# ScalarE makes the first-layer activation two units ahead, before the unit's messages; raw rounding and constant rows come after the messages

## The reference

```python
h = relu(layernorm(x))                       # no weights
e = relu(raw @ W_e1.T + b_e1) @ W_e2.T + b_e2   # raw: (206250, 64)
edge_emb = (e * (clip(polarity, 0, 1) + 0.01)) @ W_le.T + b_le
msg  = relu(h[src] + edge_emb)
aggr = segment_sum(msg, dst, 6250)
g = (h + aggr) @ W_g1.T + b_g1
out = x + relu(layernorm(g) * ln_g + ln_b) @ W_g2.T + b_g2
```

## Time and profile before

| | |
|---|---|
| median of 3 runs | 2511.51 us |
| profiled execution / its span | 2513.17 / 2511.5 us |
| TensorE busy (matmuls) | 2341.1 us, 93% |
| VectorE busy | 1904.1 us, 76% |
| GpSimd busy | 1644.0 us, 65% |
| ScalarE busy | 1586.8 us, 63% |
| second layer, L828, TensorE | 1467.2 us |
| TensorE idle ahead of L806 (first layer) | 129.2 us |

### The profile page before, as it was taken

One profiled execution on the slowest core, in us unless ns is written; L12 is line 12 of the kernel. 1 busy time (PEld: TensorE's weight loads), 2 busy tenths in 40 slices (PEclk: granted clock), 3 DMA queues, 4 the chain that ended last, 5 costly groups with the idle time before them and its releaser, 6 DMA issues.

```text
span 2511.5 us, 34919 instructions
## 1 busy us (share of the span) xinstructions
PE 2341.1 (93%) x10492; PEld 1946.3 (77%) x10492; DVE 1904.1 (76%) x3747; ACT 1586.8 (63%) x3112; POOL 1644.0 (65%) x1679
## 2 busy tenths in 40 slices
PE   5798999999999999999999999999999999999998
PEld 4677787877887787778877787877787787787876
DVE  7677777877787777777777777777787777777776
ACT  7566666666666666666666666666666666666664
POOL 6666666666666666666666666666666666666663
PEclk9899999999999999999999999999999999999999
DMA  9444444444444444444444444444444444444442
GB/s 311 131 132 129 132 146 131 139 130 134 145 140 136 131 145 139 135 133 141 139 136 133 133 135 143 134 137 132 137 143 137 134 134 143 137 137 134 141 140 60
DMA packets 136344, 349.07 MB, mean 139 GB/s; under 512 B 32019, under 2 KB 58325, under 8 KB 136149
## 3 DMA queue, kind: packets, MB, share of 16 engines
q0 software_dynamic: 77376, 211.39, 29.6%
q1 hardware_dynamic: 58772, 135.37, 15.8%
HBM read 333.82 MB, written 12.82 MB: 138 GB/s over the span
## 4 chain that ended last, share of the span: by engine, by line
PE 50%; DVE 27%; another core or an unknown queue 9%; issue 9%; ACT 4%; POOL 1%; DVEq 0%; DMA 0%; ACTq 0%; SPq 0%
PE bank L828 29%; DVE bank L676 11%; PE bank L844 9%; DVE mhl L686 7%; PE bank L806 5%; DVE oh L665 4%; PE bank L807 4%; DVE rlo L427 3%; ACT mhl L601 1%; PE bank L875 1%; PE bank L861 1%; ACT rhi L422 1%; POOL x_sba L371 1%; ACT hh L589 1%
## 5 line engine op out<-in xcount | busy, mean ns | idle before, releaser
L578 POOL DMA_INDIRECT hx<-gather_table,sidx x1612 | 1604.9, 996 | 823.7 <-issue 400.6
L828 PE MATMUL bank<-wc,hh 128*128 128x256 f32 x6448 | 1467.2, 380 | 2.7 <-issue 2.5
L828 PEld LDWEIGHTS bank<-wc,hh 128*128 128x128 f32 x6448 | 1218.9, 191 | 179.8 <-issue 9.2
L601 ACT ACTIVATE mhl<-bank 128x512 fp32r<-128x512 f32 x806 | 482.3, 599 | 842.1 <-DVE bank L676 671.7
L676 DVE SCALAR_TENSOR_TENSOR bank<-bank,gt,hx 128x256 f32<-128x256 f32 x1612 | 683.0, 484 | 380.1 <-remote 311.1
L686 DVE SCALAR_TENSOR_TENSOR mhl<-bank,mhl 128x512 fp32r<-128x512 f32 x806 | 549.7, 689 | 26.8 <-ACT mhl L601 1.8
L806 PE MATMUL bank<-rhi,w1r 128*128 128x512 f32 x806 | 379.8, 471 | 129.2 <-ACT hh L589 81.7
L589 ACT ACTIVATE hh<-bank 128x512 f32<-128x512 f32 x806 | 441.2, 601 | 28.2 <-remote 19.4
L594 ACT COPY bank<-c 128x512 f32<-128x512 f32 x802 | 450.5, 609 | 0.0
L844 PE MATMUL bank<-mhl,oh 128*128 128x512 f32 x1612 | 444.0, 397 | 0.5 <-DVE mhl L686 0.5
L665 DVE TENSOR_TENSOR oh<-iota,slot 128x512 fp32r<-128x512 f32 x403 | 279.2, 693 | 138.6 <-PE bank L844 80.7
(11 more groups left out here) (93 smaller groups left out, 479.7 us busy)
## 6 DMA issues: line engine op xcount, KB each, us to landing
raw<-in_attr_m SPq DMA_DIRECT2D x202, 512.0 KB
hx<-gather_table,sidx POOLq DMA_INDIRECT x1612
x_sba<-in_x SPq DMA_DIRECT2D x12, 512.0 KB, 8.9
gather_table<-x_sba SPq DMA_DIRECT2D x12, 512.0 KB, 7.7
xt<-in_x SPq DMA_DIRECT2D x48, 128.0 KB
out<-xt SPq DMA_DIRECT2D x48, 128.0 KB
dst_i<-in_dst_m SPq DMA_DIRECT2D x1, 805.5 KB
sidx<-in_src_m SPq DMA_DIRECT2D x1, 805.5 KB
```

What stands on the lines that cost most here:

```text
L578: eng.indirect_dma_start(out=hx[:, u % NX, j, :], out_offset=None, in_=tables, in_offset=bass.IndirectOffsetOnAxis(ap=sidx[:, t:t + 1], ax ...
L601: eng.activation(mh[:, u % 2, 2 * q:2 * q + 2, :], LB[(2 * u + q) % 4][:, :].rearrange("p (j n) -> p j n", j=2), ACT.Relu).then_inc(r_mh, 1)
L828: last = eng.matmul(o, hh[:, u % 2, k, e0:e0 + P], wc[:, k, :], start=False, stop=(j == 1 and k == 1), skip_group_check=seeded)
```

## The change

Two instructions move ahead of the loop, and in the loop ScalarE's order becomes `hidden_high(u+2)`, [6: `lift`], `message_high(u, 0)`, `message_high(u, 1)`, `raw_high(u+4)`, `seed(u+2)`, [0: `window_out`], [4: `root`]. No instruction is added or dropped, and no other engine's program changes.

```diff
                     hidden_high(0)
                     raw_high(eng, 2)
+                    raw_high(eng, 3)
+                    hidden_high(1)
                     eng.wait_ge(s_wt, 2)
                     for u in range(UNITS):
-                        if u + 3 < UNITS:
-                            raw_high(eng, u + 3)
-                        if u + 1 < UNITS:
-                            hidden_high(u + 1)
+                        if u + 2 < UNITS:
+                            hidden_high(u + 2)
                         t = TILE_AFTER.get(u // GU - 1)
                         if u % GU == 6 and t is not None:
                             lift(t)
-                        if 1 <= u < UNITS - 1:
-                            seed(u + 1)
                         message_high(u, 0)
                         message_high(u, 1)
+                        if u + 4 < UNITS:
+                            raw_high(eng, u + 4)
+                        if u + 2 < UNITS:
+                            seed(u + 2)
                         if u % GU == 0 and u >= GU:
                             window_out(u // GU - 1)
                         if u % GU == 4 and t is not None:
```

## The result

The changed kernel takes 2571.72 us (median of 4 runs, 2571.44 to 2579.55), the kernel before 2512.87 us in the same comparison: ratio 1.0239, 95% interval 1.0216 to 1.0263. It is slower by 59 us; the forecast was 2549 us, slower by 38. The profiled execution is the longest of the four, 2579.55 us with a span of 2577.8, so the record shows about 8 us more than the median. Times in this document leave out one execution of `f3_lift_behind` (4880.7 us) that fell out of line with its other four.

A forecast was written before the change was run, and what follows sets the result against it. TensorE, busy 95% of the loop, was taken as the bound. -109 + 55 + 51 + 25 + 11 gave +33, leaned up to +38 us: 2551 on the profiled execution, 2549 us as median; range 2458 to 2608.

The forecast's parts named there:

- The wait at the first layer goes: TensorE's idle time ahead of the first layer goes because the activation runs before the messages: -109 us, bounds -60 and -129.
- I take the whole 104.1 us as gone: All idle time ahead of the first layer from 200 to 2400 us goes, and 5 us more elsewhere in the loop.
- late signal: VectorE starts `total` long after the TensorE matmuls it needs: 135 such waits in the stretch, 282.3 us, 2.1 us each.
- `down` waits for `lift`: TensorE waits at `down`, u mod 7 = 6, as lift stands behind this unit's first layer: +55 us, bounds 32 and 97.
- `turn` waits for `norm`: TensorE waits at the turn, u mod 7 = 5, as root stands behind rounding and seed: +51 us, bounds 9 and 122.
- 0.37 late signals a unit: The average rate of late signals, one in 2.7 units, used to weight the waits at the three places.
- `window_turn` waits for `window_join`: The join waits for window_out, now behind the seed: TensorE waits 1.2 us after a late signal, +25 us, bounds 0 and 70.
- Ordinary units: After a late signal, low messages end about 0.15 us behind the segment's need: 0.2 us a group, 11 us in all.
- The three waits take each other's place: First rival: a late turn gives VectorE and ScalarE time to catch up, so lift and join cost less; 2455 us, chance 0.27.
- The rival in which a prompt signal makes the change a gain: TensorE's signals are prompt: three places cost 41 us, 100 us go, 2452 us; chance within the first rival's 0.27.
- VectorE as the bound: Rival: VectorE's work plus late signals set the group's pace, 43.2 us a group, +103 us, 2614 us, chance 0.13.
- the sum 38: All terms together gave +33 us, leaned up to +38 us because late signals seemed to fall more on even units.

The follow-up runs named there:

- f3_lift_behind: The changed kernel with lift put one step further back, behind the two messages: 2687.3 us, ratio 1.055 to the kernel before on the same chip.
- the three moves: The changed kernel with lift, window_out and root moved back ahead: 2333.56 us, ratio 0.999 on a quick chip; 2550.68 us, ratio 1.0013 on a laggard chip.

## Why the prediction was right, and where it was not

The direction was right, the time 2571.7 us lies in the range (2458 to 2608), and the mechanism named is the one in the record. Step by step:

- **The wait at the first layer goes: -109 us.** In the record it is -108.6 (129.2 to 20.6). But it was not time that could be won. On the quick chips the kernel before loses nothing against a kernel in which TensorE has no gap (2336.0 against 2333.6 us), so there was nothing to take; on the laggard one the wait fell by 131 us with the time unchanged (2547.8 and 2550.7). The step that failed is "I take the whole 104.1 us as gone", as a term of time. In its place came idle time where the prediction saw none or 0.15 us after a late signal: 46.6 us more at the segment and 17.1 ahead of the second layer in the three moves, besides 29.0 at the turn and 24.6 at `down`.
- **`down` waits for `lift`: +55 us.** Place and chain right, in the changed kernel's record on all three chips. Alone on a quick chip it measures 39.8 us (window_out behind included) where the prediction's part without late signals was 32; in the changed kernel's first record 72.0 us of idle stand there.
- **`turn` waits for `norm`: +51 us.** 73.5 us in the first record, 85.1 in the later one. Without late signals it is 7.0 us, window_out included: the 9 us of the prediction's lower bound. `invert` idles 1.40 us for `root` on both kinds of chip; what the laggard adds is the late first-layer signal in front, 1.6 us in the unit shown. The size failed at "0.37 late signals a unit", an even spread: behind the first layer they stand in 52 of 53 units with u mod 7 = 4, and TensorE waits at nearly every turn, though less each time than the 2.65 us reckoned. The prediction named this as its weakest point, "which no row counts"; the trace of the kernel before holds the count. There VectorE starts a total over 0.5 us late, having idled, in 43 of 57 units with u mod 7 = 4, in 39 with 2, in 26 with 0, and in 2 to 11 with 1, 3 or 5 (22 with 6).
- **`window_turn` waits for `window_join`: +25 us.** Wrong in size: VectorE waits for window_out 1.5 us each time, as said, but TensorE only 5.2 us in all. The late signals fall in few units with u mod 7 = 0 of this kernel (9 of 57), which fits; that a turn or a `down` that has just waited leaves the join early enough, the first rival's mechanism, may add to it and is not shown.
- **Ordinary units: +11 us.** 24.2 us at the segment, the low messages being its releaser, as named.
- **Rivals.** "The three waits take each other's place" was given 0.27 with 2455 us. Its time is wrong; a part of its point holds on the laggard chip, where 101.6 us of idle time went from two places and 73.8 us from the time. The rival in which a prompt signal makes the change a gain (2452 us) fell on the quick chips: without any late signal the change is slower there too, by 42.1 us. Its 41 us for the three places are met; its gain of 100 us is not there, since with prompt signals the kernel before had no wait to lose either. That is what the prediction should have seen: 282.3 us of late signals and the 104.1 us of waits are one thing, and without the first there is no second. VectorE as the bound did not come about: it is busy 74%, and idles 228.1 us ahead of its totals.

So the sum 38 stands against 59 measured, and that it came so near is in part luck. Its costs of the three places, 131 us, are 73.8 us where they were measured on a laggard chip; its gain, 98 us with the ordinary units' 11 taken off, is none there (the three moves take 2.9 us more than the kernel before). Both are too large, and they cancel. What holds is the direction and its cause: on either kind of chip undoing the three moves brings the changed kernel back to the kernel before, within 3 us.

On the quick chip the whole change is two terms over the three moves, 39.8 + 7.0 = 46.8 us; the three moves are 2.4 us quicker than the kernel before, which leaves 44.4 us by the variants against 42.1 measured. Window_out is counted in both terms; its share was not measured.

The sentence of the Trainium skill that the prediction drew on (Perfetto Trace Analysis, "Tensor Engine Instruction (MATMUL, LD_WEIGHTS)": the end of a matmul in the record is an estimate, the semaphore goes out on PSUM's acknowledgement) agrees with what the records show on the laggard chips, where VectorE started late by 376.5 us in all with nothing else to wait for. It does not say why the acknowledgement should be late on one chip and not on another, and no run here shows it.

**Open:** what the late signals are. TensorE's own pace on that chip (P) and the other engines' traffic (Q) are not told apart. That time did not change when the waits went, while TensorE's busy time grew by 25 us (an estimated 8 of them the clock), speaks for P; it is argued, not shown. Nor is it known why the late signals fall on the units with u mod 7 = 2, 4 and 6. How much of the 73.8 us on the laggard chip is `down` and how much the turn was not measured separately.

## What to carry to other kernels

A step that an engine takes ahead of its turn puts everything behind it in a new place: before moving it, list who waits for each step now standing behind it, and whether that chain starts at the same engine in the same unit. TensorE to ScalarE (activation, then lift) and back to TensorE within 0.93 us of other work costs the whole rest of the chain, 0.70 us in each of 46 tiles, whatever slack the pipeline has elsewhere. And a wait that goes away in the record is no gain until the time falls: here 131 us of it went with the time unchanged, and idle time stood at the steps behind instead. Where a forecast needs how often something falls on a given step, count it by step in the trace: an average over all steps, 0.37 a unit here, hid a place that had it nearly every time.

## What the runs showed of the hardware

The same kernel took 2336 us on three chips, and 2512.9 and 2547.8 us in two other comparisons, 7.6 to 9.1% more, each within 0.3% from execution to execution. The granted TensorE clock is lower on the laggards, 0.991 in the first profile and 0.981 to 0.989 on the other against 0.995 to 0.997 on the quick chips, all for the kernel before; but a difference of about 1% does not make 7.6 to 9.1%. What marks them is waits released by "remote", ahead of VectorE's totals 311.1 and 376.5 us in the two profiles of the kernel before, and none at all in any record of the quick kind. Why a chip is of the one kind or the other, no run shows. A difference between two kernels must come from one chip, and its size belongs to that chip: this change costs 1.8% on the quick kind and 2.4 and 2.9% on the other.
